# A decoder layer on one core: the beginning of its schedule in another order

## What is computed

```python
def circulant(x, c, b):
    y = irfft(rfft(x) * rfft(c)); return y + b
Q, K, V = circulant(x, wq_c, wq_b), circulant(x, wk_c, wk_b), circulant(x, wv_c, wv_b)
out = circulant(merge(softmax(Q K^T * 8 ** -0.5) V), wo_c, wo_b)
x = layernorm(x + out)
Sim = (x @ w1)[:, :, None] + (ctx @ w2)[:, None, :] + einsum(x * w3, ctx) + b_sim
hq_hat = softmax(Sim, 2) @ ctx; hc_bar = softmax(max(Sim, 2), 1) @ x
x = layernorm(x + concat(x, hq_hat, x * hq_hat, x * hc_bar) @ W_qv + b_qv)
x = layernorm(x + routed_experts(x) + shared_expert(x))
```

## Time and profile before

| | us |
|---|---|
| median of 3 runs | 440.55 |
| lowest, highest | 437.79, 444.63 |
| the profiled execution | 441.29 |
| its span, first to last instruction | 439.6 |
| busy: PE, DVE, POOL, ACT | 340.5, 285.2, 192.7, 176.6 |
| mean granted clock of TensorE | 0.913 of full speed |

### The profile page before, as it was taken

One profiled execution on the slowest core, in us unless ns is written; L12 is line 12 of the kernel. 1 busy time (PEld: TensorE's weight loads), 2 busy tenths in 40 slices (PEclk: granted clock), 3 DMA queues, 4 the chain that ended last, 5 costly groups with the idle time before them and its releaser, 6 DMA issues.

```text
span 439.6 us, 8430 instructions
## 1 busy us (share of the span) xinstructions
PE 340.5 (77%) x2365; PEld 222.0 (51%) x2365; DVE 285.2 (65%) x842; ACT 176.6 (40%) x498; POOL 192.7 (44%) x377
## 2 busy tenths in 40 slices
...
GB/s 100 167 180 85 220 94 111 157 241 143 188 76 150 222 86 108 32 102 28 41 50 99 2 18 18 50 13 80 74 60 44 45 43 44 48 44 24 25 192 95
DMA packets 53198, 39.56 MB, mean 90 GB/s; under 512 B 7624, under 2 KB 46633, under 8 KB 53148
## 3 DMA queue, kind: packets, MB, share of 16 engines
...
## 4 chain that ended last, share of the span: by engine, by line
PE 52%; DVE 14%; DMA 9%; issue 9%; SPq 6%; POOL 4%; ACT 3%; another core or an unknown queue 1%; ACTq 0%; POOLq 0%; DVEq 0%
PE pT L1469 9%; PE pS L1469 8%; PE pM L1480 4%; PE pT L1446 3%; PE pO L1460 2%; PE pT L1301 2%; PE pM L1277 2%; PE pS L1470 2%; PE pT L1470 2%; PE pO L1314 2%; DVE negmax L908 2%; PE pS L1291 2%; DMA X<-in_x 2%; DMA Qst<-parts_scr 2%; PE pO L1318 1%
## 5 line engine op out<-in xcount | busy, mean ns | idle before, releaser
L687 POOL DMA_INDIRECT ys<-sim_rhs,row_dest x39 | 40.8, 1046 | 41.6 <-ACT sim_rhs L842 39.7
L908 DVE TENSOR_REDUCE negmax<-pS 128x4 f32<-128x512 f32 x64 | 43.2, 680 | 20.4 <-PE pS L1291 20.2
L742 ACT ACTIVATE PT<-pT 128x512 f32<-128x512 f32 x64 | 38.1, 595 | 42.6 <-PE pT L1301 41.7
L1291 PE MATMUL pS<-Kdiag,Qst 128*128 128x512 f32 x64 | 42.5, 673 | 15.0 <-DMA Qst<-parts_scr 14.6
L1469 PE MATMUL pT<-W,XH 128*128 (+1 forms) x94 | 51.1, 626 | 0.0
L1469 PE MATMUL pS<-W,XH 128*128 (+1 forms) x94 | 49.0, 603 | 0.0
L1039 DVE TENSOR_TENSOR PT<-pT,PT 128x512 f32<-128x512 f32 x47 | 32.4, 689 | 24.2 <-PE pT L1470 17.9
L587 POOL TENSOR_SCALAR vareps<-meanvar 128x1 f32<-128x1 f32 x32 | 7.4, 232 | 88.6 <-DVE meanvar L937 88.3
L826 ACT COPY XH<-pO 128x384 f32<-128x384 f32 x47 | 22.5, 479 | 47.5 <-PE pO L1462 42.7
L1480 PEld LDWEIGHTS pM<-W,XH 128*128 128x128 f32 x188 | 28.0, 191 | 21.0 <-issue 17.4
L609 POOL DMA_INDIRECT xs<-X,slot x32 | 33.7, 1053 | 8.3 <-issue 6.0
...
## 6 DMA issues: line engine op xcount, KB each, us to landing
...
```

The costliest lines, as they stand in the source:

```text
L687: pool.indirect_dma_start(ys.ap(), bass.IndirectOffsetOnAxis(ap=row_dest[:, k:k + 1], axis=0), YO[:, i % RING, :], None).then_inc(s_ysc[i ...
L742: act.activation(PT[:, u % 3, :], pT[:, 0, :], ACT.Exp, scale=SCALE).then_inc(p_sb, 1)
L908: dve.tensor_reduce(out=negmax[:, b % 2, HG * j:HG * (j + 1)], in_=pS[:, u % 2, :].rearrange("p (g k) -> p g k", g=HG), axis=AX.X, op=ALU.max,
L1291: pe.matmul(pS[:, u % 2, :], Qst[:, (b // 2) % 2, j, (b % 2) * P:(b % 2 + 1) * P], Kdiag[:, b % 2, j, :, :], start=True, stop=True).then_i ...
```

## The change

- SP: query and key circulants are written and read first (`circ_read(0)`), X of group 0 between; value and output circulants come in a second transfer. The whole-context load and the three repeated bias rows and the repeated gate bias go; four short rows are loaded into `one_row` instead, and X of group 1 directly after the small loads.
- PE: each circulant half is a product of its own, the second after the key projection of group 0, which has pT as its bank. One product of `ones` and `one_row` spreads all bias rows; ACT copies them to `wide_rows`.
- The context is loaded in four transfers (slots -1, 7, 19, 35) and transposed in slots 4, 20, 36, 52, in pM, after `front(n)`; DVE and ACT read it there, after their own `front(n)`. The gate's weights are transposed in slot 3.
- Group 1's three steps go from slots -4, -3, 0 to -2, -1, 0, both its spills to slot 1. In SP's list `q_stack` comes ahead of `k_diag`.
- PE issues products of `ones` by `ones` into pO (`warm`), which nothing reads: 10 at the start, 6 after the transposes of group 0, 2 after the first circulant product, 30 after the bias rows, 2 after each scores of the slots before 0, and 4 in slot 0.

The diff, without the declarations of semaphores, a few reordered memsets and uses of the renamed bias rows:

```diff
@@ -38,11 +38,16 @@
 GROUP_STEPS = {-4: 0, -3: 1, 0: 2}
+SECOND_GROUP_STEPS = {-2: 0, -1: 1, 0: 2}
+SPILL_SLOTS = (-2, 1)
+SECOND_SPILL_SLOTS = (1, 1)
 FIRST_SLOT, LAST_SLOT = -G4 * U - 4, 72
...
 MIDDLE = (5, 6)
-PREP_SLOT = -11
-X_SLOTS = {-7: 1, 1: 2, 9: 3}
+GATE_SLOT = 3
+CONTEXT_SLOT = 4
+CONTEXT_LOADS = {-1: 0, 7: 1, 19: 2, 35: 3}
+X_SLOTS = {1: 2, 9: 3}
 SHARED_SLOT, SHARED_SLOTS = 25, 18
@@ -60,6 +65,7 @@
 FFN_SLOT = 67
+WARM_UP, WARM_CIRC, WARM_COPY, WARM_STACKS, WARM_SCORES, WARM_MAX = 10, 6, 2, 30, 2, 4
 EARLY_TILES = ROUTE_SLOT + G4 * U * (NG - 2) + ROUTE_STEPS - 1
@@ -99,10 +105,9 @@
 qk_bias = sb("qk_bias", [P, 2])
-bv_row = sb("bv_row", [P, D])
-bo_row = sb("bo_row", [P, D])
-bqv_row = sb("bqv_row", [P, D])
-gateb_row = sb("gateb_row", [P, E])
+wide_rows = sb("wide_rows", [P, 3 * D + E])
+bv_row, bo_row, bqv_row = (wide_rows[:, k * D:(k + 1) * D] for k in range(3))
+one_row = sb("one_row", [1, 3 * D + E])
 ctx_sb = sb("ctx_sb", [NC1, B, D])
...
@@ -322,9 +326,18 @@
     for g in range(NG):
-        if n - G4 * U * (g - 1) in GROUP_STEPS:
-            return g, GROUP_STEPS[n - G4 * U * (g - 1)]
+        steps = SECOND_GROUP_STEPS if g == 1 else GROUP_STEPS
+        if n - G4 * U * (g - 1) in steps:
+            return g, steps[n - G4 * U * (g - 1)]
     return None
...
+def context_step(n):
+    q, r = divmod(n - CONTEXT_SLOT, G4 * U)
+    return q if r == 0 and 0 <= q < NG else None
...
+def projection_bank(g, k):
...
+    return pT[:, 0, :] if (g, k) == (0, 2) else pM[:]
@@ -353,9 +366,19 @@
 def _(sp):
-    for k, c in enumerate((wq_c, wk_c, wv_c, wo_c)):
+    def circ_source(k, c):
         sp.dma_start(circ_scr.ap()[k].rearrange("(r n) -> r n", r=2),
-                     bass.AP(c.tensor, 0, [[0, 2], [1, D]])).then_inc(s_circw, 16)
+                     bass.AP(c.tensor, 0, [[0, 2], [1, D]])).then_inc(s_circw if k < 2 else s_qkb, 16)
...
+    def circ_read(half):
+        sp.wait_ge(s_circw, 32)
+        if half == 1:
+            sp.wait_ge(s_qkb, 64)
+        sp.dma_start(hankel[:, 2 * half:2 * half + 2, :],
+                     bass.AP(circ_scr, 4 * D * half + 1, [[1, P], [2 * D, 2], [1, D]])).then_inc(s_circ[half], 16)
...
+    circ_source(0, wq_c)
+    circ_source(1, wk_c)
@@ -364,17 +387,18 @@
-    sp.wait_ge(s_circw, 64)
-    sp.dma_start(hankel, bass.AP(circ_scr, 1, [[1, P], [2 * D, 4], [1, D]])).then_inc(s_circ, 16)
-    sp.dma_start(ctx_sb[1:NC1], ctx_1024.rearrange("b j d -> j b d")).then_inc(s_ctx, 16)
-    sp.wait_ge(c_zero, 2)
-    small = [(bv_row[:], bass.AP(wv_b.tensor, 0, [[0, P], [1, D]])), (bo_row[:], bass.AP(wo_b.tensor, 0, [[0, P], [1, D]])),
-             (bqv_row[:], bass.AP(b_qv.tensor, 0, [[0, P], [1, D]])), (gateb_row[:], bass.AP(gate_b.tensor, 0, [[0, P], [1, E]])),
-             (wqv[:], W_qv.rearrange("(k p) n -> p k n", p=P)),
+    circ_source(2, wv_c)
+    circ_source(3, wo_c)
+    circ_read(0)
+    circ_read(1)
+    sp.wait_ge(c_zero, 3)
+    small = [(one_row[:, D * k:D * k + r.shape[0]], r.rearrange("(o n) -> o n", o=1)) for k, r in enumerate((wv_b, wo_b, b_qv, gate_b))]
+    small += [(wqv[:], W_qv.rearrange("(k p) n -> p k n", p=P)),
              (bsim[0:1, :], b_sim.rearrange("(p o) -> p o", o=1)), (gw_sb[:], gate_w)]
...
         sp.dma_start(to, src).then_inc(s_small, 16)
+    load_x(1)
@@ -455,18 +479,21 @@
         for g in range(NG):
-            if n == G4 * U * (g - 1) - 2:
-                spill(g, 0)
-            if n == G4 * U * (g - 1) + 1:
-                spill(g, 1)
+            for i, at in enumerate(SECOND_SPILL_SLOTS if g == 1 else SPILL_SLOTS):
+                if n == G4 * U * (g - 1) + at:
+                    spill(g, i)
         if n in X_SLOTS:
             load_x(X_SLOTS[n])
+        if n in CONTEXT_LOADS:
+            q = CONTEXT_LOADS[n]
+            sp.dma_start(ctx_sb[1:NC1, G4 * q:G4 * q + G4, :],
+                         ctx_1024[G4 * q:G4 * q + G4].rearrange("b j d -> j b d")).then_inc(s_x[q], 16)
         if n >= -3 and n % U == 1 and (n + 3) // U < B:
             max_rows((n + 3) // U)
+        if n % (2 * U) == 6 and 0 <= (n + 10) // (2 * U) < B // 2:
+            q_stack((n + 10) // (2 * U))
         if n % U == 2 and 0 <= (n + 10) // U < B:
             k_diag((n + 10) // U)
-        if n % (2 * U) == 6 and 0 <= (n + 10) // (2 * U) < B // 2:
-            q_stack((n + 10) // (2 * U))
         if n % (2 * U) == 0 and 0 <= n // (2 * U) + 1 < B // 2:
@@ -535,11 +562,10 @@
 def _(pool):
+    pool.memset(ones[:], 1.0).then_inc(c_zero, 1)
+    pool.memset(ident[:], 0.0).then_inc(c_ident, 1)
+    pool.memset(flip, 0.0).then_inc(c_flip, 1)
     pool.memset(bsim[:], 0.0).then_inc(c_zero, 1)
-    pool.memset(ident[:], 0.0).then_inc(c_ident, 1)
-    pool.memset(ctx_sb[0:1], 0.0).then_inc(c_pad, 1)
-    pool.memset(flip, 0.0).then_inc(c_flip, 1)
-    pool.memset(ones[:], 1.0)
     pool.memset(pad_row[:], 0.0).then_inc(c_zero, 1)
...
@@ -636,12 +663,12 @@
             if b == 0:
-                pool.wait_ge(s_small, 16 * SMALL)
+                pool.wait_ge(gwT_sb, 1)
             if b % G4 == 0:
...
                 pool.wait_ge(r_sb, b - 1)
-            pool.tensor_tensor(XB[:, b % 2, :], X[:, b, :], bo_row[:], ALU.add).then_inc(xb_sb, 1)
+            pool.tensor_tensor(XB[:, b % 2, :], X[:, b, :], bo_row, ALU.add).then_inc(xb_sb, 1)
         for g in range(SG):
@@ -716,7 +743,7 @@
         act.wait_ge(sr_sb, q + 1)
-        act.activation(sim_add[:, 4 * q:4 * q + 4, :], pX[:, q % 2, 0:4 * NC1].rearrange("p (b j) -> p b j", b=4)[:, :, 1:NC1],
+        act.activation(sim_add[:, 4 * q:4 * q + 4, :], pM[:, 0:4 * NC1].rearrange("p (b j) -> p b j", b=4)[:, :, 1:NC1],
                        ACT.Identity, bias=bsim[:], scale=wsim[:, 1:2]).then_inc(cT_sb, 1)
@@ -728,12 +755,15 @@
             if g == 0 and k == 1:
-                act.wait_ge(s_qkb, 32)
+                act.wait_ge(s_qkb, 64)
             act.wait_ge(qk_ps, 2 * g + i + 1)
...
                 act.wait_ge(s_parts[i], 48 * g)
-            act.activation(qk_hi[:, i, :], pM[:], ACT.Identity, bias=qk_bias[:, i:i + 1],
+            act.activation(qk_hi[:, i, :], projection_bank(g, k), ACT.Identity, bias=qk_bias[:, i:i + 1],
                            scale=1.0).then_inc(hi_sb, 1)
+            if (g, k) == (0, 2):
+                act.wait_ge(gwT_ps, 1)
+                act.copy(wide_rows[:], pX[:, 0, 0:3 * D + E]).then_inc(gwT_sb, 1)
@@ -851,13 +881,13 @@
     for n in range(FIRST_SLOT, LAST_SLOT + 1):
-        if n == PREP_SLOT:
...
-            act.wait_ge(gwT_ps, 1)
+        if n == GATE_SLOT:
...
+            act.wait_ge(gwT_ps, 2)
             act.copy(gwT[:], pX[:, 1, 0:E]).then_inc(gwT_sb, 1)
-            for q in range(4):
-                context(q)
         front(n)
+        if context_step(n) is not None:
+            context(context_step(n))
         for g in range(NG - 1):
@@ -882,25 +912,32 @@
         dve.wait_ge(cT_ps, q + 1)
-        dve.tensor_scalar(sim_rhs[:, 4 * q:4 * q + 4, :], pX[:, q % 2, 0:4 * NC1].rearrange("p (b j) -> p b j", b=4)[:, :, 1:NC1],
+        dve.tensor_scalar(sim_rhs[:, 4 * q:4 * q + 4, :], pM[:, 0:4 * NC1].rearrange("p (b j) -> p b j", b=4)[:, :, 1:NC1],
                           wsim[:, 2:3], wsim[:, 0:1], ALU.mult, ALU.add).then_inc(sr_sb, 1)
...
+    def circulants(half):
+        dve.wait_ge(circ_ps, half + 1)
+        dve.tensor_copy(circ[:, 2 * half:2 * half + 2, :].rearrange("p k n -> p (k n)"), pX[:, half, 0:2 * D]).then_inc(circ_sb, 1)
...
             dve.wait_ge(hi_sb, 2 * g + i + 1)
-            dve.scalar_tensor_tensor(out=qk_lo[:, i, :], in0=pM[:], scalar=qk_bias[:, i:i + 1],
+            dve.scalar_tensor_tensor(out=qk_lo[:, i, :], in0=projection_bank(g, k), scalar=qk_bias[:, i:i + 1],
                                      in1=qk_hi[:, i, :].bitcast(F32), op0=ALU.add, op1=ALU.subtract).then_inc(lo_sb, 1)
+            if (g, k) == (0, 2):
+                circulants(1)
...
             dve.wait_ge(c_v, 1)
+            dve.wait_ge(gwT_sb, 1)
         if b >= 2:
...
         dve.tensor_tensor(to, pM[:, 0:D].rearrange("p (g j d) -> p g j d", g=HG, j=U),
-                          bv_row[:].rearrange("p (g j d) -> p g j d", g=HG, j=U), ALU.add).then_inc(v_sb, 1)
+                          bv_row.rearrange("p (g j d) -> p g j d", g=HG, j=U), ALU.add).then_inc(v_sb, 1)
...
@@ -1205,15 +1242,12 @@
     dve.memset(Kdiag[:].bitcast(F32), 0.0).then_inc(c_kdiag, 1)
-    dve.wait_ge(circ_ps, 1)
-    dve.tensor_copy(circ[:].rearrange("p k n -> p (k n)"), pX[:, 0, :]).then_inc(circ_sb, 1)
     dve.memset(Vz[:], 0.0).then_inc(c_v, 1)
+    circulants(0)
     for n in range(FIRST_SLOT, LAST_SLOT + 1):
-        if n == PREP_SLOT:
-            dve.wait_ge(s_small, 16 * SMALL)
-            for q in range(4):
-                context(q)
         front(n)
+        if context_step(n) is not None:
+            context(context_step(n))
         for g in range(NG - 1):
@@ -1250,16 +1284,22 @@
 def _(pe):
```

(66 more changed lines are left out.)

10 lines of the change are left out of this document (5 added, 5 removed).

## The result

The change made the kernel slower: 452.9 us (median of four, 450.3 to 454.9) against 441.1 (437.8 to 444.6), a ratio of 1.028 [1.0215, 1.0344]. Medians are of all runs of a kernel, the ratios, with their 95% intervals, of its faster runs alone. The forecast was 440.5 with a range of 430 to 448. The profiled execution took 450.31 us, with a span of 448.5; before, 441.29 and 439.6.

What follows compares the result with a forecast made beforehand. What counts is how much earlier attention ends; SP's issuing binds 40.69 to 73.35 us. The terms -10.6 + 9.75 + 0.8 = -0.05, on the median of 440.55, gave 440.5 us, range 430 to 448.

Steps and rivals of the forecast that it cites:

- A: Start up to the scores of unit 0: earlier loads and a faster clock bring them from 30.41 to 22.8, -7.6 us.
- B: From there to unit 4's transposed scores: 56.85 becomes 45.3 or 47.4, mean -10.6 us, bounds -7 and -13.
- C: Contexts in slots 4, 20, 36, 52: the maxima's transpose waits until ACT has read pM; +9.75 us, bounds 0 and 12.
- rival B: PE standing at each context lets the clock fall; four falls add 7 to 12 us: 448 to 452; chance 0.08.
- D: Small things: context load in slot 7 +0.5, gate transpose and copy in slot 3 +0.3, other loads and group 1 0.
- A fell: Rival: the context stalls are covered, only DVE's 0.77 is paid per context (3.1 in all): 433.9 us; chance 0.27.
- C fell: Rival: thirty start fillers at half speed hold unit 0's scores to 29.9 against 22.8: 446.5 us; chance 0.10 with Rival D.
- Rival D: At the start SP's small loads, X and parts contend: +2 to +4, 443.5 us; sign: parts landing after 21.

Runs made afterwards that it cites:

- run in slot 3: The changed kernel with all four contexts in slot 3, in the two pX banks, and the context loaded whole in slot -4: 435.0 us, ratio 0.983.
- gap fillers: The kernel of the run in slot 3 plus unread PE products in five gaps (slots 17, 33, 37, 49, 53): 428.7 us, ratio 0.975.
- run with group 1 early: The kernel of the run in slot 3 with group 1's steps and spills back in their old slots: 436.7 us, ratio 0.994.
- fillers in the stall: The changed kernel plus unread PE products before the maxima's transpose in slots 5, 21, 37 and 53: 445.8 us, ratio 1.0135.

## Why the prediction was wrong

**The front (A and B) was right up to unit 4, and not beyond.** Its gain was put at 10.6 us and was 10.3. The sum then carried it whole to the end of attention. The run in slot 3, free of the context stalls, keeps 9.1 us of it at unit 5, 8.4 at unit 36, 5.2 at unit 56 and 5.9 at the end; by the medians 6.0. So some 4 of 10 us are given back, most of it between units 36 and 56. That run has the clock at half for 64.8 us, the kernel before for 51.2, and with the gap fillers and 37.6 us at half the gain is 12.4 at unit 63. That fits a front whose gain is given back in falls of the clock, as does the run with group 1 early, but the gap fillers would also help a kernel that lost it in another way, and in the kernel before they help by 0.5% only. It is argued, not shown.

**The context (C) had the right mechanism and half the price.** PE waits at the maxima's transpose until ACT has read pM, in four slots, released by the instruction that was named. The forecast was 9.75 us (2.7, 2.85, 1.6 and 2.6), the steps grew by 4.2, 3.0, 4.5 and 2.9, and the whole cost 17.6 to 17.9. By the landmarks of the change, the sum was 4.9 us short in the steps (14.7 against 9.75) and 3.3 short for what lies between them, where it had nothing. Three things are in the difference:

- The clock. The step that failed first is the sum of C: it had no term for the falls. They stood only in rival B, at 7 to 12 us and a chance of 0.08, though the prediction had the row that shows one (a granted 0.50 at 94 to 100, behind three microseconds with hardly any work on PE) and the stalls of 2 to 3 us that would bring them. The fillers in the stall measured 7.1 us for those of slots 20, 36 and 52. That is against the change; against the kernel before, which has falls of its own at other places, the change loses only 3.3 us outside the four steps. Rival B's condition, three falls of four that would not have come, was met: the kernel before has a granted 1.00 over 44 to 60, 155 to 163 and 213 to 221, and the change has falls in all three; only around slot 20 had the kernel before a short one of its own (0.93 over 100 to 108). The forecast's time with the foot of B on it is 447.5; the median was 452.9. B's top of 452 comes near it by luck in part: B added 7 to 12 us of falls to steps that were themselves 4.9 us too short.
- Slot 36. Here a term was mis-sized. The wait was 3.6 us by the prediction's own formula (160.9 less the transpose's start at 157.27), and only 1.6 was counted, because the residual sum on DVE comes later there and the rest was to be absorbed. Nothing was: the step grew by 4.5 (by 3.8 with the contexts alone in the kernel before), and of it 0.8 was back at unit 52. The attention output also came 0.8 us later behind the start of the slot (156.51 less 151.49, before 159.31 less 155.09). DVE stood for 1.52 us shortly before it, and the profile names no engine of this core that ended that wait.
- Slot 4. In the kernel before the step with a context takes 4.8 us, in the change 6.0. The windows show the difference: in the change the slot runs at a granted 0.50. That fall isn't the context's. It came while PE waited 4.76 us for the maxima's transfer to unit 4's diagonal, which can be read as the front's own gain seen from PE: what is pulled forward waits for the transfer behind it. No rival had this wait in it.

Slots 20 and 52 were sized rightly (2.85 and 2.6 against 3.0 and 2.9).

The Trainium skill, "TensorE: Matmul & The Clock Gate", section "HAM oscillation — how this bites in real kernels", prices such falls at the time at half clock times one half. Its rule that waits between bursts bring them held in every context slot. Its price is too high here: from 81.9 us at half clock in the change to 51.2 with the fillers in the stall it gives 15.4 us, and 7.1 were measured. PE's own work became shorter by 12.0 us (355.7 us busy in the change; 353.0 with the fillers, of which 9.3 are the fillers), so a part of the 15.4 was waiting, and some 5 of the 12.0 turned into waits elsewhere. Other runs say it more strongly: the kernel without start fillers has 100.6 us at half clock, the one with them 81.9, and the two take the same time.

**D and rivals A, C and D.** The small things can't be told from zero. A fell: the stalls were not covered. C fell: the thirty fillers (60 instructions) took 6.96 us, full speed, and the scores of unit 0 began 0.5 us after the forecast. Rival D fell: SP issued the key diagonals, which wait for the last key parts, at 20.20, so these landed by then (forecast 18.8, the sign for D 21).
